# Half-precision adjacency tiles by casting transfers from GpSimd instead of a ScalarE cast

## The reference

```python
deg = jnp.sum(adj, axis=1, keepdims=True) + 1e-05
adj_norm = adj / deg
h_neigh = adj_norm @ h
out = h_neigh @ W_neigh.T + b_neigh + h @ W_self.T + b_self
return jax.nn.relu(out)
```

## Time and profile before

| | |
|---|---|
| median of 3 runs | 1331.69 us (1330.75 to 1333.65) |
| the profiled execution | 1323.42 us |
| its span, from the first to the last instruction | 1321.8 us |
| TensorE busy | 1106.8 us (84%) |
| VectorE busy | 861.4 us (65%) |
| ScalarE busy | 631.1 us (48%) |
| GpSimd busy | 122.9 us (9%) |
| mean granted TensorE clock | 0.92 of full speed |

### The profile page before, as it was taken

How to read it: one execution, slowest core, us unless ns; L and a number is a source line. 1 busy time by engine, 2 the same in 40 slices (tenths; PEclk the granted TensorE clock), 3 DMA queues, 4 the chain that set the end, 5 groups by cost and what they waited for, 6 DMA issues and landing times. The chain is left out here.

```text
span 1321.8 us, 24385 instructions
## 1 busy us (share of the span) xinstructions
PE 1106.8 (84%) x7322; PEld 898.9 (68%) x7323; DVE 861.4 (65%) x1887; ACT 631.1 (48%) x723; POOL 122.9 (9%) x135
## 2 busy tenths in 40 slices
PE   4759999999998979699748999996059999999940
PEld 3548888888897868588636888885026666666630
DVE  6479999999973562764674366667235556556526
ACT  2669999999953433133135444541023323323310
POOL 1000000000000000000000013222301211211210
PEclk9889999999997789899979999998579999999975
DMA  9937777777401303223234888771261111111117
GB/s 281 285 118 218 244 221 217 237 234 222 129 1 34 103 2 130 68 65 129 68 119 150 352 293 329 268 242 36 91 275 55 52 52 56 52 52 56 52 62 268
DMA packets 73189, 195.53 MB, mean 148 GB/s; under 512 B 8289, under 2 KB 58336, under 8 KB 62784
## 3 DMA queue, kind: packets, MB, share of 16 engines
q1 hardware_dynamic: 55776, 163.61, 37.0%
q0 software_dynamic: 9232, 18.52, 5.2%
q10 hardware_dynamic: 8144, 12.91, 2.7%
HBM read 141.28 MB, written 53.74 MB: 148 GB/s over the span
## 5 line engine op out<-in xcount | busy, mean ns | idle before, releaser
L586 PE MATMUL PS<-G,PT 128*128 128x256 f16 x2028 | 230.3, 273 | 0.0
L586 PEld LDWEIGHTS PS<-G,PT 128*128 128x128 f16 x2028 | 198.7, 98 | 22.9
L1196 PE MATMUL sum<-H,adjTh 128*128 128x257 f16 x676 | 153.6, 275 | 4.5 <-ACT adjTh L1162 4.5
L1198 PE MATMUL sum<-H,adjTh 128*128 128x256 f16 x676 | 153.7, 274 | 0.0
L1590 DVE SCALAR_TENSOR_TENSOR hb<-ePsH,w_unscale,eb 128x1024 f32<-128x1024 f32 x59 | 75.8, 1284 | 89.8 <-PE ePsH L1511 89.8
L1511 PE MATMUL ePsH<-W,xT_hi 128*128 x472 | 122.4, 382 | 4.8 <-DVE xT_lo L1581 4.8
L1531 PE MATMUL ePsY<-W,actT 128*128 x472 | 111.6, 380 | 0.2 <-issue 0.2
L573 PE MATMUL PS<-ident,probs 128*128 128x128 f32 x676 | 90.0, 280 | 22.2 <-DVE PT L434 20.5
L1547 ACT ACTIVATE xT_hi<-ePsX 128x256 f16<-128x256 f32 x59 | 22.6, 384 | 177.7 <-PE ePsX L1500 177.7
L887 PE MATMUL psH<-HT,w 128*128 128x256 f32 (+1 forms) x416 | 97.2, 391 | 11.5 <-ACT G L938 10.4
L434 DVE SCALAR_TENSOR_TENSOR PT<-PS,PT 128x1024 f16<-128x1024 f32 x104 | 103.6, 1018 | 4.4 <-ACT PT L283 4.4
(11 more groups left out here) (237 smaller groups left out, 1769.8 us busy)
## 6 DMA issues: line engine op xcount, KB each, us to landing
adjf<-adj_dram SPq DMA_DIRECT2D x26, 1664.0 KB, 8.0
adjTf<-adjT_dram SPq DMA_DIRECT2D x26, 1664.0 KB, 8.4
slot_rows<-blank SPq DMA_DIRECT2D x26, 1028.0 KB, 10.8
stage<-eW_dram SPq DMA_DIRECT2D x8, 1024.0 KB, 6.8
w_parts<-parts SPq DMA_DIRECT2D x8, 1024.0 KB, 4.6
W<-w_parts SPq DMA_DIRECT2D x8, 1024.0 KB, 10.5
xs<-slot_rows SPq DMA_DIRECT2D x59, 128.5 KB, 2.0
results<-results_dram ACTq DMA_DIRECT2D x12, 512.0 KB, 9.3
```

The lines of the kernel that those rows point to most:

```text
L586: mm = nc.tensor.matmul(acc[u][:, 0:D], left, right, start=(j == 0 and n == 0), stop=(j == T - 1 and n == 2))
L1196: nc.tensor.matmul(acc[u][:, 0:D + 1], left, H[:, j, 0:D + 1], start=(j == 0), stop=False, skip_group_check=True)
L1198: mm = nc.tensor.matmul(acc[u][:, 0:D], left, H[:, j, D + 2:2 * D + 2], start=False, stop=(j == T - 1), skip_group_check=True)
```

## The change

The tiles are no longer loaded as float32 by SyncE and cast by ScalarE. GpSimd issues transfers whose source is float32 and whose destination is float16, straight into one tensor `adjTh` with four tile buffers (as many bytes for each partition as the two float32 buffers had; the two float16 buffers beside them are gone). The first four are issued at the start of the self projection (argument `ahead`), where GpSimd had nothing to do; tile i from 4 on is issued when the products of tile i-4 are done. TensorE waits for the transfer itself. The expert weights stay on SyncE, weight e waiting until the products of 2e tiles are done. The loops over pairs of `mean_aggregation` are written out for all engines.

```diff
@@ normalised_projection
+        if ahead is not None:
+            @block.gpsimd
+            def _(pool):
+                ahead(pool)
@@ mean_aggregation, SyncE
-            def load_pair(i, with_weights):
-                for u in range(2):
-                    if not (isinstance(i, int) and i + u < 2):
-                        wait(sp, half_ready, i + u - 1)
-                        sp.dma_start(adjf[u][:, :], adjv[i + u, :, :]).then_inc(adj_in[u], 16)
...
+            for e in range(E1):
+                wait(sp, acc_ready, 2 * e)
+                sp.dma_start(flat[:, e * part:(e + 1) * part], dram["w1_parts"][:, e, :]).then_inc(W1_in, 16)
@@ ScalarE
-            def half(t, u):
-                act.wait_ge(adj_in[u], 8 * (t - u) + 16)
-                wait(act, acc_ready, t - 1)
-                nc.scalar.copy(adjh[u][:, :], adjf[u][:, :]).then_inc(half_ready, 1)
@@ TensorE
             def products(t, u):
-                pe.wait_ge(half_ready, t + 1)
+                pe.wait_ge(adj_in[t % 4], 16 * (t // 4) + 16)
                 wait(pe, agg_ready, t - 1)
                 for j in range(T):
-                    left = adjh[u][:, j * P:(j + 1) * P]
+                    left = adjh[:, t % 4, j * P:(j + 1) * P]
...
-            tile_pairs(pe, body, FIRST, LAST, TOTAL)
+            for i in range(0, TOTAL, 2):
+                body(i)
@@ GpSimd
+            def load(i):
+                if 4 <= i < T:
+                    pool.wait_ge(acc_ready, i - 3)
+                    pool.dma_start(adjh[:, i % 4, :], adjv[i, :, :]).then_inc(adj_in[i % 4], 16)
...
-            body(0)
-            with pool.Fori(2, T - 1, 2) as i:
-                body(i)
+            for i in range(0, T + 8, 2):
+                load(i + 2)
+                load(i + 3)
+                if i >= 8:
+                    scatter(i - 8)
@@ gnn_program
-                t["adjTf"] = [agg.enter_context(nc.sbuf_tensor(f"adjTf{u}", [P, NP], F32)) for u in range(2)]
-
-                def first_tiles(sp):
-                    for u in range(2):
-                        sp.dma_start(t["adjTf"][u][:, :], dram["adjT"][u, :, :]).then_inc(t["adj_in"][u], 16)
+                t["adjTh"] = agg.enter_context(nc.sbuf_tensor("adjTh", [P, 4, NP], F16))
+
+                def first_tiles(pool):
+                    for i in range(4):
+                        pool.dma_start(t["adjTh"][:, i, :], dram["adjT"][i, :, :]).then_inc(t["adj_in"][i], 16)
```

More of the change, by code:

```diff
@@ L631, in _, with normalised_projection @@
             steps(pe, iteration, FIRST, LAST, TOTAL)
-def normalised_projection(nc, t, name, w_dram, width, out, bias=None, HT=None, H=None, after=None):
+def normalised_projection(nc, t, name, w_dram, width, out, bias=None, HT=None, H=None, after=None, ahead=None):
     with ExitStack() as ctx:
@@ L1078, in mean_aggregation @@
         stats_done = sem("d_stats")
-        adjf = t["adjTf"]
-        adjh = [sb(f"adjTh{u}", [P, NP], F16) for u in range(2)]
+        adjh = t["adjTh"]
         Wn = sb("Wn", [P, KD, D])
@@ L1110, in mean_aggregation @@
         adj_in, W1_in = t["adj_in"], t["W1_in"]
-        w_in, half_ready, ones_set = sem("d_w"), sem("d_half"), sem("d_ones")
+        w_in, ones_set = sem("d_w"), sem("d_ones")
         acc_ready, deg_ready, rdeg_ready, agg_ready = sem("d_acc"), sem("d_deg"), sem("d_rdeg"), sem("d_agg")
@@ L1123, in mean_aggregation @@
         adjv = dram["adjT"]
-        FIRST, LAST, TOTAL = 6, T, T + 6
+        TOTAL = T + 6
         def live(t):
@@ L1135, in _ @@
                 sp.dma_start(to[...], dram[name]).then_inc(w_in, 16)
-            def load_pair(i, with_weights):
-                for u in range(2):
-                    if not (isinstance(i, int) and i + u < 2):
-                        wait(sp, half_ready, i + u - 1)
-                        sp.dma_start(adjf[u][:, :], adjv[i + u, :, :]).then_inc(adj_in[u], 16)
[L1142 to L1153, removed]
+            flat = t["W1"][:, :, :, :, :].rearrange("p e k h n -> p (e k h n)")
+            part = KD * 2 * 2 * F1
+            for e in range(E1):
+                wait(sp, acc_ready, 2 * e)
+                sp.dma_start(flat[:, e * part:(e + 1) * part], dram["w1_parts"][:, e, :]).then_inc(W1_in, 16)
             sp.wait_ge(w_in, 16 * 8)
@@ L1169, in body @@
             def body(i):
-                if live(i):
-                    half(i, 0)
                 if live(i - 2):
@@ L1176, in body @@
                     nc.scalar.activation(std[:, :], moments[:, :, 1], ACT.Sqrt, bias=eps[:, :]).then_inc(std_ready, 2)
-                if live(i):
-                    half(i + 1, 1)
                 if live(i - 2):
@@ L1186, in _ @@
             act.wait_ge(ones_set, 1)
-            tile_pairs(act, body, FIRST, LAST, TOTAL)
+            for i in range(0, TOTAL, 2):
+                body(i)
         @block.tensor
@@ L1390, in body, with scatter @@
                     write_slots(i - 6)
-            tile_pairs(dve, body, FIRST, LAST, TOTAL)
+            for i in range(0, TOTAL, 2):
+                body(i)
         @block.gpsimd
         def _(pool):
-            def body(i):
+            def load(i):
+                if 4 <= i < T:
+                    pool.wait_ge(acc_ready, i - 3)
+                    pool.dma_start(adjh[:, i % 4, :], adjv[i, :, :]).then_inc(adj_in[i % 4], 16)
+            def scatter(i):
                 settled(pool, scatter_waits, (rows_ready, 4 * i + 8))
@@ L1711, in gnn_program @@
         t["W1_in"] = ctx.enter_context(nc.semaphore("W1_in"))
-        t["adj_in"] = [ctx.enter_context(nc.semaphore(f"adjT_in{u}")) for u in range(2)]
+        t["adj_in"] = [ctx.enter_context(nc.semaphore(f"adjT_in{u}")) for u in range(4)]
         with ExitStack() as experts:
@@ L1717, in gnn_program @@
                 t["own"] = agg.enter_context(nc.sbuf_tensor("own", [P, T, D], F32))
-                t["adjTf"] = [agg.enter_context(nc.sbuf_tensor(f"adjTf{u}", [P, NP], F32)) for u in range(2)]
-                def first_tiles(sp):
-                    for u in range(2):
-                        sp.dma_start(t["adjTf"][u][:, :], dram["adjT"][u, :, :]).then_inc(t["adj_in"][u], 16)
+                t["adjTh"] = agg.enter_context(nc.sbuf_tensor("adjTh", [P, 4, NP], F16))
+                def first_tiles(pool):
+                    for i in range(4):
+                        pool.dma_start(t["adjTh"][:, i, :], dram["adjT"][i, :, :]).then_inc(t["adj_in"][i], 16)
                 normalised_projection(nc, t, "self", dram["WsT"], D, t["own"], bias=(dram["b_self"], dram["b_neigh"]),
-                                      H=t["H"], after=first_tiles)
+                                      H=t["H"], ahead=first_tiles)
                 mean_aggregation(nc, t, dram)
```

## The result

The changed kernel takes 1333.82 us (median of 20, 1328.16 to 1337.46), the kernel before 1331.18 us (median of 20, 1326.65 to 1333.86). The ratio is 1.0023, 95% interval 1.0012 to 1.0034. So the change makes the kernel 3 to 4 us slower, where 1331 us and "no difference" had been forecast.

What follows compares the result with a forecast made beforehand. TensorE was taken to set the pace from 714.21 us on, leaving the aggregation's start to win. From the median, 1331.7 - 2.96 (cast wait) - 1.63 (clock) + 4 (bias delay) = 1331.1, said as 1331; range 1326 to 1342.

Steps and rivals of the forecast that it cites:

- the bias row: Sign: VectorE's bias sum in the self projection moves 4 us from 676.4; wrong if under 2 or over 7.
- the delay of the biases: Start of self projection: biases land later because of GpSimd's tiles, 4 us taken, middle 3 to 6, bounds 0 and 14.
- rival 3: Start of self projection: biases wait for most of the four tiles, delay 8 to 14 us, 1335 to 1341; chance 0.17.
- The rule that the prediction weighed and did not take: DMA engines alternate queues packet by packet; at the self projection's start this would cost the biases up to 8 us.
- The gain: Aggregation's start: first product 2.96 us sooner without the cast wait, plus 1.63 from the clock staying up; 4.6 us.
- The casts: Aggregation: TensorE sets the pace, so taking casts off ScalarE gives nothing for each pair.
- The loops: Aggregation: writing the loops out is worth 0 to 0.1 us for each pair at most; nothing taken.
- The casting row: Aggregation transfers: a casting tile row takes 0.54 us, hidden; above 0.82 us transfers bind.
- rival 4: Aggregation: the cast is paid by element, so transfers bind above 0.82 us a row; 1345 or 1376; chance 0.16.
- The odd and even tiles' loads: Aggregation, GpSimd: even loads behind scatters have 18.7 us of cover; odd loads wait without holding the scatters up.
- The DMA share of a pair: Sign in the aggregation: transfers fill about 0.8 of a pair.
- The prediction's weighing of VectorE against GpSimd's descriptors: Aggregation: by the skill's rule each issue takes some 2.5 us more, 5 a pair, still covered; trace does not agree.

Runs made afterwards that it cites:

- e5: The changed kernel run again, unchanged; ratio 1.0032 to the kernel before.
- e4: The changed kernel with three early drains on GpSimd inside the aggregation; 1327.89 us, ratio 0.9986 to the kernel before.
- e6: The changed kernel, but GpSimd issues one tile at once and three after the projection's loads have landed; 1325.43 us, ratio 0.9998.
- e3: The kernel before, its first two plain float32 tiles issued by ScalarE at the start of the self projection; 1337.77 us, ratio 1.0069.
- e1: The changed kernel, but GpSimd waits for self_W and both biases before issuing the first four tiles; 1325.87 us, ratio 0.9975.
- e2: The kernel before with only the aggregation's loops over pairs written out; 1328.78 us, ratio 1.0002.
- e9: The kernel before run again, unchanged; ratio 1.0001.
- e10: The kernel before with written-out loops and three early drains on GpSimd in the aggregation; 1326.28 us, ratio 0.9970.
- e8: The changed kernel with the projection's loads ahead of the first four tiles and three early GpSimd drains; 1315.91 us, ratio 0.9924.
- e7: The changed kernel with biases ahead of the tiles, and TensorE waiting for the aggregation's small loads before the first product; 1327.70 us, ratio 1.0022.
- e11: The kernel before, with tile 0 cast by ScalarE at the end of its self projection work; 1330.59 us, ratio 0.9999.
- e12: The kernel before with tile 0's early cast, written-out loops and three early GpSimd drains; 1326.12 us, ratio 0.9971.

## Why the prediction was wrong

It ended on the wrong side because two terms were not what the sum had: one was sized too low, from a wrong picture of how the two queues share the engines, and one was missing. The first is what its own list of signs names: the bias row moved by more than 7 us.

**The failed step: the delay of the biases.** The prediction took 4 us, with 3 to 6 as the middle and 14 as the upper bound, from the reading that "the latecomer waits for what is queued and then alternates", and that "the first bias and `self_W` are likely ahead". Measured: 9.03 us; in e5 8.1 to 8.4 and in e4 9.2 to 9.5, by which kernel before is taken. `self_W` was ahead. The first bias was not: GpSimd's issue (674.02) came in the same 10 ns as SyncE's of it (674.03), and the biases took turns with tile rows from the beginning, 304 packets against 289. So the wait that the earlier trace rows had shown for a scatter does not carry over; here nothing waited for a whole tile, and nearly all rows of both biases paid a turn of 0.51 us, where the prediction counted the second bias's eight. The scatter's wait had also been read as longer than it was: by the raw records of the kernel before its first packet comes 4.14 us behind the issue at 778.00, but 1.54 us behind each first scatter of a group from 899 us on, when no tile moves. So 1.5 us of it is the scatter's own, and 2.6 us are a wait. In the prediction's terms the size is that of rival 3, whose mechanism (biases behind most of four tiles) did not happen: e6 and e3 show 4 us for each tile that is in the way, and the change shows 9 for four, where the small rows are the fewer. The rule that the prediction weighed and did not take, that of the Trainium skill (DMA: Bandwidth & Descriptors, section "Queues, rings and completion order"), is round robin packet by packet, and the trace agrees: 304 packets against 289 in 10 us. The prediction worked out up to 8 us by it, 16 bias rows at 0.51 us, where 8.1 to 9.5 were measured.

**The missing term: 1.8 us at the stage's end.** Nothing in it asked what GpSimd does with 22 more transfers after the last of them. The prediction priced their issue alone, and that is nothing on the path. The trace of before held the stretch, 7.85 us from the last scatter to the next stage.

**Right.** The gain: 4.6 us forecast, 4.52 measured, 2.9 of it the pause (4.50 to 1.60) and 1.6 the clock (7.62 to 6.01 from the first product to `degree`). The 0.5 us that the table has in the projection can't be told from scatter: from the bias row to the end of the projection it was 33.3 to 33.7 us in before, e1, e2, e5, e9 and e10, with the late bias row (e5, 33.45) and without, and 34.3 in e6 and e8. The clock there stood at 0.50 from 687.0 to 692.6 behind the longer wait, where in the kernel before the 5.6 us from its bias row on had a mean of 0.62; what that cost, no run isolates:

```profile
687.00:692.60 5.60, 4.40 (x13) 3.24 (x14) 3.53 (x9) 2.19 (x7) 0.00 (x0) 0.50 1.04 216
```

The casts are worth nothing for each pair: right, 184.17 against 184.18. The loops nothing: right, e2. The casting row: taken at 0.54 us, to decide from 0.82; by the raw records a row is one packet with 6,656 bytes written and takes 512 ns, about as long as the plain read of a tile's row (498 ns), so rival 4 is out. The odd and even tiles' loads hidden behind the scatters: right, TensorE has no wait for `adjTh<-adjT_dram`. Their issue was sized too high, 1.53 us for 0.53 to 0.60, and without effect. The DMA share of a pair came out at 0.72, for about 0.8. GpSimd's rows in one pair:

```profile
776.85 0.53 POOL L1385 DMA_DIRECT2D adjTh<-adjT_dram  x1 [6.79 <-PE sum L1182]
784.31 1.02 POOL L1392 DMA_INDIRECT slot_rows<-rows,slot_i  x1 [6.93 <-DVE slot_i L1358]
...
789.19 0.60 POOL L1385 DMA_DIRECT2D adjTh<-adjT_dram  x1
```

VectorE was busy for 9.71 of the 15.15 us of a pair. The prediction's weighing of VectorE against GpSimd's descriptors (the Trainium skill, SBUF — State Buffer, section "SBUF: two separate sides", 3,100 ns for 620) stands: the trace does not agree for this work, with the casting transfers too. Whether any of VectorE's instructions here ran in one of the two-port modes that the section speaks of, no row tells.

**Together**: -4.5 + 0.5 + 9.0 + 1.8 = +6.8 us by the traces. By the medians it is +3.1 (0.0023 x 1331) and +4.2 in the second set. e5's profile against e9's gives 655.3 - 650.8 = +4.5. What lies between the traces and the medians, 0.3 to 3.7 us, is open. The same comparison for the experiments, by ratio and by the time behind S against the 650.0 of before: e1 -3.3 and -3.8, e3 +9.2 and +9.2, e8 -10.1 and -8.3, e2 +0.3 and +0.1, e10 -4.0 and -3.4, but e6 -0.3 and +2.1, e7 +2.9 and +5.6, e11 -0.1 and +3.7, e12 -3.9 and -1.5, and e4 -1.9 and +2.0. Each kernel has one profile, so a size of 2 to 4 us is told by the ratios alone, and the rows tell where it lies.

## What to carry to other kernels

A transfer that is moved to an idle queue is not free for the small loads that are issued beside it: each small row can pay for one whole row of the big one, on every DMA engine. Price it as the number of rows for each engine, of the small loads or of the big transfer, whichever is fewer, times the time of a large row, and let the big transfer wait for the small ones' semaphore; it cost nothing here and turned a loss of 0.2% into a gain of 0.25%. Count what an engine must still finish at a barrier, too: transfers on GpSimd that look free in its stage come back at its end, and early `drain`s in idle time took 0.3% off this kernel even without the change (e10). And when a first wait is shortened, look at the third and fourth item of the pipeline: if their loads are issued no sooner, the gain is given back there.

## What the runs showed of the hardware that was not expected

- GpSimd's DRAIN at a barrier took 83 ns for each transfer of 128 rows that it had issued (52, 74, 59 of them: 4.31, 6.10, 4.87 us; 4 of them: 0.37). A drain with transfers still moving lasts longer: by the raw records the one at the end of the self projection, behind the four tiles just issued, took 19.8 us and ended 0.5 us behind their last packet (694.58), and the early ones, 5.8 to 8.6 us, ended 1.2 to 2.0 us behind the last packet of GpSimd's queue. Both were hidden.
- GpSimd's indirect transfer, 0.97 us of issue, had its first packet 1.54 us after the issue began when no tile moved, and 4.1 to 4.3 us after it when float32 tiles moved on SyncE's queue (kernel before).
- A transfer that casts float32 to float16 runs at the rate of a plain one by bytes read: 512 against 498 ns for 13,312.
- The granted clock fell to 0.50 after pauses of TensorE between the stages of 2.65 (e11), 4.50 (before) and 6.54 us (e7), and in e11 once more after a wait of 2.10 us inside the stage; it stayed at 1.00 after pauses of 1.60 (after, e1, e6, e8). Whether the pause alone decides, no run here tells.
- The stages ahead of the change, with the same code, ended anywhere between 670.95 and 677.96 us. What makes them vary is open.
